# Own attention: reciprocal and product behind the step's last maximum on VectorE; cross attention: values of the next batch in other steps

## What is computed

```
x = _ln(xx, ln1_g, ln1_b)
x = x + _mha(x, x,  a1_..., causal=True)     # "own": 256 keys
x = _ln(x, ln2_g, ln2_b)
return x + _mha(x, ee, a2_..., causal=False)  # "cross": 1601 keys

# inside _mha, after layer norms and projections
a = softmax(einsum('bhsd,bhtd->bhst', q, k) * D ** -0.5)
if causal: a = a * mask                       # mask after the softmax: s < t only
o = einsum('bhst,bhtd->bhsd', a, v)
x_out = x + o @ li1_w + li1_b
```

## Time and profile before

| | |
|---|---|
| median of 3 runs | 7793.97 us (7776.19 to 7797.02) |
| the profiled execution | 7805.02 us |
| its span | 7803.3 us |
| TensorE busy in the span | 6932.4 us (89%) |
| VectorE busy | 5893.4 us (76%) |
| ScalarE busy | 4967.2 us (64%) |
| GpSimd busy | 2320.7 us (30%) |
| mean granted TensorE clock | 0.942 of full |

### The profile page before, as it was taken

The page is one execution under the profiler, slowest core; times in us unless marked ns, Lnnn a source line. Parts: engine busy times, 40 slices in busy tenths (PEclk is TensorE's granted clock), DMA queues, the critical chain, the costliest instruction groups (busy, mean ns, idle before and its releaser), DMA issues. The chain is left out here.

```text
span 7803.3 us, 186325 instructions
## 1 busy us (share of the span) xinstructions
PE 6932.4 (89%) x73814; PEld 3133.2 (40%) x73814; DVE 5893.4 (76%) x12885; ACT 4967.2 (64%) x9846; POOL 2320.7 (30%) x2368
## 2 busy tenths in 40 slices
PE   6999999977999998788769999999997789999979
PEld 2333333353333333344424444444444433333335
DVE  6888888856989987677657777777775379989955
ACT  4777888734888885444335656656654158888842
POOL 1222222111122120244435555555555112122100
PEclk9999999987999999788879999999999689999989
DMA  4444443104443431000100000000001153443400
GB/s 99 90 99 95 92 89 85 42 28 97 87 96 75 102 89 25 28 15 17 37 24 10 6 10 9 7 10 7 6 3 45 31 109 84 86 97 74 98 23 14
DMA packets 319830, 417.82 MB, mean 54 GB/s; under 512 B 56533, under 2 KB 238054, under 8 KB 318969
## 3 DMA queue, kind: packets, MB, share of 16 engines
q1 hardware_dynamic: 317432, 405.36, 23.0%
q10 hardware_dynamic: 1536, 0.53, 0.0%
HBM read 225.41 MB, written 174.66 MB: 51 GB/s over the span
## 5 line engine op out<-in xcount | busy, mean ns | idle before, releaser
L688 ACT ACTIVATE a_probs<-scores_ps 128x512 f32<-128x512 f32 (+2 forms) x5248 | 2821.3, 591 | 358.5 <-PE scores_ps L608 266.4
L747 DVE TENSOR_REDUCE a_unit_max<-bank 128x1 f32<-128x512 f32 x3072 | 2003.5, 683 | 180.0 <-PE bank L595 145.5
L625 PE MATMUL bank<-a_probs,a_v_sb 128*9 128x256 f32 (+1 forms) x20992 | 1615.9, 380 | 29.3 <-ACT a_out_sb L695 20.3
L1294 ACT ACTIVATE cross_probs<-scores_ps 128x512 f32<-128x512 f32 (+1 forms) x1792 | 869.5, 571 | 602.2 <-PE scores_ps L1189 601.7
L608 PE MATMUL scores_ps<-a_stack 64*128 64x256 bf16 (+1 forms) x10496 | 1131.5, 275 | 63.1 <-ACT a_probs L688 55.8
L747 DVE TENSOR_REDUCE a_unit_max<-scores_ps 128x1 f32<-128x512 f32 x1536 | 1049.8, 683 | 162.4 <-PE scores_ps L595 145.2
L1376 DVE TENSOR_REDUCE cross_unit_max<-bank 128x1 f32<-128x512 f32 x1536 | 981.7, 685 | 245.8 <-PE bank L1175 242.6
L595 PE MATMUL bank<-a_stack 63*128 63x512 bf16 (+2 forms) x3413 | 1039.2, 372 | 5.8 <-DVE a_unit_max L747 1.3
L1460 POOL TENSOR_TENSOR cross_added<-cross_probs 128x1024 f32<-128x1024 f32 x384 | 905.8, 2359 | 395.9 <-PE bank L1222 330.7
L608 PEld LDWEIGHTS scores_ps<-a_stack 64*128 64x128 bf16 (+1 forms) x10496 | 373.1, 96 | 994.8 <-ACT a_probs L688 833.8
L512 POOL CAST a_parts<-a_qk 128x512 bf16<-128x512 f32 (+3 forms) x225 | 118.0, 525 | 1893.7 <-ACT a_qk L707 1814.1
(11 more groups left out here) (421 smaller groups left out, 9975.2 us busy)
## 6 DMA issues: line engine op xcount, KB each, us to landing
a_stack_dram<-a_parts SPq DMA_DIRECT2D x288, 400.2 KB, 4.3
a_stack<-a_stack_dram SPq DMA_DIRECT2D x256, 348.2 KB, 8.1
a_stack<-a_stack_dram SPq DMA_DIRECT2D x128, 444.2 KB, 9.8
a_ctxT<-in_ctxT SPq DMA_DIRECT2D x48, 400.2 KB, 5.0
a_stack_dram<-a_parts SPq DMA_DIRECT2D x288, 64.0 KB, 2.6
a_stack_dram<-a_parts SPq DMA_DIRECT2D x96, 128.0 KB, 2.7
f_x<-x_after_dram SPq DMA_DIRECT2D x32, 256.0 KB, 3.3
x_after_dram<-a_res SPq DMA_DIRECT2D x48, 128.0 KB, 4.6
```

What stands on the lines that cost most here:

```text
L625: ins = pe.matmul(out_bank[32 * h:32 * h + V8, q0:TOK], v[0:n, e.t, 4 * e.g + h, :], A.probs[0:n, held, o + q0:o + TOK], start=(e.t == 0), ...
L688: act.activation(by_pair(A.probs[0:n, b, a * 512:(a + 1) * 512])[:, :, q0:TOK], by_pair(score_bank[(2 * e.i + a) % 3][0:n, :])[:, :, q0:TO ...
L747: ins = dve.tensor_reduce(unit_max[:, e.g % 2, qt, 2 * a + j, c:c + 1], bank[:, 0:e.s.chunks[c][1]], AX.X, ALU.max)
L1294: act.activation(probs[0:n, b, h, 0:m, :].rearrange("p m q -> p (m q)"), score_bank[h][0:n, 0:m * TOK], ACT.Exp, scale=scale).then_inc(S[" ...
```

## The change

For the own attention (`s.own`) the `norm` event is put behind the units of part 2 instead of straight behind `take`; cross keeps its place. Only VectorE acts on `norm`, so only its order changes: reduce of unit 3, `negmax`, reciprocal, product, then slot 2.

For cross, the seven `v` events move from steps 3, 9, 10, 16, 17, 23, 24 to 1, 8, 10, 15, 17, 22, 24; `ctx` from 15 and 22 to 16 and 23; `proj` from step 2 to step 3, slot 2 in both. The numbers of instructions stay.

```
-            put(15, 1, "ctx", j=0)
+            put(16, 1, "ctx", j=0)
             put(19, 2, "x_turned")
-            put(22, 1, "ctx", j=1)
-        for j, i in enumerate((3, 9, 10, 16, 17, 23, 24)):
+            put(23, 1, "ctx", j=1)
+        for j, i in enumerate((1, 8, 10, 15, 17, 22, 24)):
             prepare(i, 1, True, "v", j=j)
...
-        proj_at = (2, 2)
+        proj_at = (3, 2)
...
             if steps[k][1] == per_quad - 1:
-                plan += [Ev("take", g=steps[k][0], i=zero + k), Ev("norm", g=steps[k][0], i=zero + k)]
+                plan.append(Ev("take", g=steps[k][0], i=zero + k))
+                norm = [Ev("norm", g=steps[k][0], i=zero + k)]
+                if not s.own:
+                    plan += norm
         plan += by_part[2]
+        if pv and s.own:
+            plan += norm
```

## The result

The changed kernel takes 7705.14 us in the median of 6 runs (7679.04 to 7746.06), the kernel before 7791.49 (6 runs, 7775.87 to 7797.02): ratio 0.9894, 95% interval 0.9873 to 0.9915. The profiled execution took 7682.31 us, span 7680.6, among the shortest of its kernel; before it was 7805.02, longer than any of its six runs.

What follows compares the result with a forecast made beforehand. A chain of stages: own paced by the TensorE-VectorE loop, cross by TensorE, busy 112.80 of 121.50 us. Own's 15 plus cross's 21 make 36 us off: 7769 us profiled, 7758 median; range 7722 to 7792.

Steps and rivals of the forecast that it cites:

- Own's new order: Own: VectorE does reduce, `negmax`, reciprocal, product; idle about 1.3 us before the reduce; TensorE waits 0.9 or more for `unit_max`.
- What own's order saves: Own, VectorE's four steps: 0.22 + 0.54 + 0.22 + 0 = 1.0 us a batch, 15 us in all.
- the delay d of the reciprocal: Own: later start of VectorE's reciprocal, 0.59 us in steps 0 and 2, 0.27 in step 1, near 0.8 in step 3.
- step 3, gain near 0: Own's step 3, at half clock: matmul about 0.2 us longer, reciprocal's delay near 0.8 us, so gain near 0.
- Own clock 0.82: Own: the granted clock stays at its mean of 0.82; any other value would show the prediction wrong.
- the first rival: Own's clock recovers: all batches run as the 34.33 us one, 38 us more saved, 7720 us; chance 0.12.
- Cross's waits: Cross, TensorE: values wait 0.4 us, units behind the product 1.0, transposes 1.14; no 0.99 before scores of steps 2 and 9.
- Cross's sum: Cross: TensorE's waits fall from 7.1 to 5.9 us, given as 1.3 us a batch, 21 us in 16.
- Nothing outside these: Outside own's and cross's changed places: everything stays as before, and later `proj` and context transposes cost nothing.
- The fourth rival: Cross: reciprocal starts 1.06 us later, cross loses 27 us, total 7806 us, no difference; chance 0.08.
- The second and third: Waits only change places: 12 us off, 7782 us, chance 0.22; own falls deeper into half clock: 7827 us, chance 0.08.

Runs made afterwards that it cites:

- the first series: The changed kernel measured once more, beside the kernel before on the same chip: 7687.58 us, ratio 0.9856.
- the kernels with fillers: Own's projection matmuls issued repeatedly: in every step of the kernel before, 0.9968; in the changed kernel's step 2, 0.9846; also its step 1, with cross transposes moved, 0.9825.
- two fillers: Changed kernel, own's projections issued three times in step 2 and twice in step 1, cross's context transposes at steps 15 and 22, slot 2: 7659.42 us, 0.9825.
- one filler: Changed kernel, own's step 2 projections issued three times: 7673.78 us; also with cross's context transposes at steps 15 and 22, slot 2: 7662.61 us.
- the addition short: Changed kernel with own's layer norm pieces in slot 1 and GpSimd's own addition cut to 32 of 256 columns: 7667.06 us in one run.

## Why the prediction was right and wrong

The signs and the places were right, the size was too small by more than half. Step by step:

- **Own's new order**: right. No matmul waits for `negmax`, and unit 2's wait is 0.77 us and more (for "0.9 and more"). The idle ahead of the reduce is 1.25 (for 1.3). The stall did move down the step as said.
- **What own's order saves** was mis-sized: 0.22 + 0.54 + 0.22 + 0 = 1.0 us a batch, 15 in all, against 0.37 + 0.65 + 0.34 + 0.51 = 1.87 and 30 at equal clock. The form of the sum held: 0.81 less the delay d of the reciprocal. Its d was too large. From unit 3 to the reciprocal it is 3494.41 - 3493.17 = 1.24 us after, 3570.19 - 3569.43 = 0.76 before, so d = 0.48 and not 0.59, which gives 0.33 (the forecast let 0.19 us pass from the start of `negmax` to the reciprocal, where its own rows have 0.09 to the next work, 3573.13 - 3573.04, and the trace after has 0.09 too); in step 1 it is 1.24 against 3577.30 - 3576.22 = 1.08, d = 0.16 and not 0.27, which gives 0.65. The largest miss is "step 3, gain near 0": its d was taken from a stretch at half clock. At full clock step 3 is like step 0 (d = 0.47, which gives 0.34); the 0.17 that it gains beyond that are not explained.
- **"Own clock 0.82"** was wrong. It is 0.93 in the profile and 0.91 in the next. This is the first rival, which had 0.12: it asked for batches of 34.33 at 0.90; they came at 30.86 (1.00) to 34.7. In the profiled pair it makes 69.6 - 30 = 40 us. It differs from run to run, and the spread of 67 us goes with it: the three runs from 7679 to 7684 us have a mean clock over the program of 0.950 or 0.951, the three from 7726 to 7746 have 0.941 to 0.943. Of the medians' 86 us, 47 are cross's and 30 own's order, so 9 are left to the clock and the rest; of the 118 in the first series, 41 are. That TensorE's waits bring the half clock is shown by the kernels with fillers, which put work into the waits and leave what runs at full clock as long as it was (three steps in the old order, the batch in the new). In the old order own's clock rose from 0.82 to 0.93; in the new order, with two fillers, it is 0.98, without one such stretch between the third batch and the fourteenth. The fillers take idle time away and add work at once, so they can't say which of the two counts. What exactly tips a batch into a stretch at 1.2 GHz stays open: the batches of 30.86 and 34.15 us with one filler come from the same order. The rule that the prediction took from the Trainium skill, "TensorE: Matmul & The Clock Gate", section "A second HAM failure mode: psum-queue depth-cycling", that frequent small idles between groups make the clock swing between its two levels, agrees with these traces.
- **Cross's waits**: right in place and nearly in size. Values wait 0.30 (for 0.4), units behind the product 0.99 (for 1.0), transposes 1.09 and 1.14 (for 1.14), and the 0.99 before the scores is gone. They add up to 4 x 0.30 + 2 x 0.99 + 1.09 + 1.14 = 5.4 us (for 5.9) from 7.1, 1.7 a batch.
- **Cross's sum** is the step that failed: "5.9 us against 7.1, so 1.3 us a batch, 21 us". (5.9 against 7.1 is 1.2 by its own numbers, or 20 us in 16.) A batch lost 2.96 us, 47 in all, since the sum held only waits that the view lists. The bank of the values' second half, which VectorE's copy of 0.69 us holds up in a step of four units, was 0.37 us in each of four steps and in no row. 1.7 + 1.5 = 3.2 us, against 2.96 measured; the 0.2 too much are not explained. The step lengths of before would have shown it: steps 3, 10 and 17 took 4.56 us each, and their TensorE groups of two units 0.75 to 0.78 us where steps without a copy of values or keys have 0.38 or 0.39, with no wait listed.
- **Nothing outside these**: nearly so. 122.7 - 69.6 - 47.4 = 5.7 us are left, of which 4.8 lie ahead of own's first transpose of `negmax` (3227.90 for 3232.66), where the change touches nothing.
- The fourth rival (the reciprocal slips by the whole of the values) did not come: the unit's 0.99 excludes it. The second and third did not either.

With 30 and 47 in place of 15 and 21 the forecast would have been 7794 - 77 = 7717 (77 being 30 + 47), 12 us above the result and 5 under the range; these 12 are put down to the clock, and no run measures them by themselves.

## What to carry to other kernels

Sum a moved step by the length of whole steps, not by the waits that a view lists: compare a step's length with that of its neighbours that do the same work, and look behind a difference with no wait beside it for a bank or buffer that is held inside a merged group. In a loop that runs between two levels of the clock, price an order at the full clock, and carry the clock's recovery as a term of its own with a wide bound. Before an event is moved, look at every engine that has a part in it, and at what these engines will then do at the same time: moving the layer norm moved GpSimd's addition onto VectorE's product.

## What the runs showed of the hardware

- VectorE's 128x256 product of two SBUF operands takes 0.42 us alone and up to 2.43 us under GpSimd's addition of 2.35 us, and ends right behind it; with the addition short, its longest is 0.52. The Trainium skill, "SBUF — State Buffer", section "Who interferes with whom", says that a VectorE instruction with two SBUF inputs and a GpSimd instruction that reads SBUF exclude each other for a whole instruction, by the order of issue. The traces agree.
- Work added to TensorE inside its waits made the kernel before faster: ratio 0.9968 [0.9952, 0.9984], with own's granted clock at 0.93 instead of 0.82. For the changed kernel it is less sure. Own takes 503.84 us at 0.96 and 514.51 at 0.93 in the two profiles with one filler, 502.91 at 0.98 with two, against 514.00 at 0.93 and 522.81 at 0.91 without; of the ratios 0.9846 [0.9825, 0.9867] lies clear of the first series of the changed kernel and overlaps its second, 0.9856 [0.9835, 0.9877].
